# Turning a router product round inside a software-pipelined sweep: weights stationary, both halves of a tile in one moving operand, the result one step later

## What is computed

```python
# channel mixing, then the second residual's norm
r2 = sigmoid(einsum('btc,dc->btd', xr2, cm_Wr))
k2 = square(relu(einsum('btc,dc->btd', xk2, cm_Wk)))
x  = x + r2 * einsum('btc,dc->btd', k2, cm_Wv)
x  = x0 + ga * x                                  # residual, gated
h  = layernorm(x) * (1 + cb) + sb                 # "h3" in the kernel
# router of the experts
logits = einsum('bsd,ed->bse', h, Wr)             # 8 experts
scores = softmax(logits); topk_scores, topk_idx = top_k(scores, 2)
out = gb * (shared(h) + routed(h, topk_scores, topk_idx)) + x
```

## Time and profile before

| | |
|---|---|
| Time, median of 3 runs | 1969.69 us (1968.26 to 1974.74) |
| Span of the profiled execution | 1967.3 us |
| PE busy | 1751.4 us, 89% of the span |
| DVE busy | 1323.2 us, 67% |
| ACT busy | 716.7 us, 36% |
| POOL busy | 575.9 us, 29% |
| Channel mixing, 543 to 845 us | PE 276.67 us busy of 302, DVE 268.78, mean granted clock 0.89 |

### The profile page before, as it was taken

The page is one execution under the profiler, slowest core; times in us unless marked ns, Lnnn a source line. Parts: engine busy times, 40 slices in busy tenths (PEclk is TensorE's granted clock), DMA queues, the critical chain, the costliest instruction groups (busy, mean ns, idle before and its releaser), DMA issues.

```text
span 1967.3 us, 29963 instructions
## 1 busy us (share of the span) xinstructions
PE 1751.4 (89%) x9188; PEld 1523.2 (77%) x9188; DVE 1323.2 (67%) x2361; ACT 716.7 (36%) x1146; POOL 575.9 (29%) x691
## 2 busy tenths in 40 slices
PE   4599999997899999997999999999999999999800
PEld 0488888885777777776899999998999999999800
DVE  4899999965898898877432333326666666666566
ACT  2344444443433343333111111115554554554322
POOL 0343333323776676643144410000000000000076
PEclk8799999998998888887999999999999999999955
DMA  8333333327544334322455521105667767667387
GB/s 322 115 122 116 116 116 116 116 84 255 199 145 149 133 134 144 128 89 83 148 181 186 185 92 43 43 22 187 240 231 248 241 230 248 238 232 248 108 260 252
DMA packets 140152, 321.82 MB, mean 164 GB/s; under 512 B 20184, under 2 KB 20184, under 8 KB 134864
## 3 DMA queue, kind: packets, MB, share of 16 engines
q1 hardware_dynamic: 116080, 258.94, 39.4%
q0 software_dynamic: 12800, 41.95, 6.5%
q10 hardware_dynamic: 11232, 20.45, 2.7%
HBM read 213.23 MB, written 108.05 MB: 163 GB/s over the span
## 4 chain that ended last, share of the span: by engine, by line
PE 74%; DVE 14%; POOL 4%; issue 4%; DMA 3%; ACT 1%; SPq 0%; DVEq 0%; POOLq 0%; ACTq 0%
PE bank L424 17%; PE bank L426 17%; PE bank L425 17%; DVE mix L1280 5%; PE bank L1730 5%; PE bank L1728 5%; PE bank L1729 5%; PE bank L435 4%; POOL cb_y L863 3%; PE bank L1722 2%; DVE xh L1265 2%; DVE h_lo L1335 1%; PE bank L1678 1%; DMA stage<-in_w_k 1%; PE bank L1679 1%
## 5 line engine op out<-in xcount | busy, mean ns | idle before, releaser
L424 PE MATMUL bank<-gu_hi,ex_x_hi 128*128 128x352 f32 x1136 | 382.0, 336 | 0.8 <-DVE gu_lo L1362 0.8
L426 PE MATMUL bank<-gu_hi,ex_x_lo 128*128 128x352 f32 x1136 | 369.5, 325 | 0.0
L425 PE MATMUL bank<-gu_lo,ex_x_hi 128*128 128x352 f32 x1136 | 369.2, 325 | 0.0
L863 POOL DMA_INDIRECT cb_y<-expert_out_rows,slots x64 | 69.2, 1081 | 738.9 <-DMA expert_out_rows<-y_rows 719.7
L1478 DVE TENSOR_TENSOR hid<-bank,sg_t 128x352 f32<-128x352 f32 x142 | 74.5, 525 | 307.6 <-ACT sg_t L1015 307.6
L424 PEld LDWEIGHTS bank<-gu_hi,ex_x_hi 128*128 128x128 f32 x1136 | 216.1, 190 | 1.2 <-issue 1.2
L425 PEld LDWEIGHTS bank<-gu_lo,ex_x_hi 128*128 128x128 f32 x1136 | 216.1, 190 | 0.0
L426 PEld LDWEIGHTS bank<-gu_hi,ex_x_lo 128*128 128x128 f32 x1136 | 215.2, 189 | 0.0
L1015 ACT ACTIVATE sg_t<-bank 128x352 f32<-128x352 f32 x142 | 65.8, 464 | 396.6 <-PE bank L426 396.6
L1728 PE MATMUL bank<-dn_hi,hid_hi 128*128 128x512 f32 x426 | 168.0, 394 | 3.1 <-DVE hid_lo L1482 3.1
L1730 PE MATMUL bank<-dn_hi,hid_lo 128*128 128x512 f32 x426 | 168.2, 395 | 0.0
(11 more groups left out here) (214 smaller groups left out, 3999.8 us busy)
## 6 DMA issues: line engine op xcount, KB each, us to landing
raw<-in_ex_gu SPq DMA_DIRECT2D x39, 1408.0 KB, 6.6
expert_in_rows<-zero_rows SPq DMA_DIRECT2D x32, 624.0 KB
raw<-in_ex_dn SPq DMA_DIRECT2D x39, 512.0 KB, 7.5
ex_x<-expert_in_rows SPq DMA_DIRECT2D x78, 256.0 KB, 2.7
expert_out_rows<-y_rows ACTq DMA_DIRECT2D x78, 256.0 KB, 2.0
h_rows<-h_t SPq DMA_DIRECT2D x64, 256.0 KB, 2.6
x_t<-in_x SPq DMA_DIRECT2D x32, 256.0 KB, 2.8
timemix_rows<-o_t SPq DMA_DIRECT2D x32, 256.0 KB, 2.0
```

The source lines that it names most:

```text
L424: pe.matmul(acc, act_hi[i], w_hi[i], start=(i == 0), stop=False)
L425: pe.matmul(acc, act_hi[i], w_lo[i], start=False, stop=False)
L426: last = pe.matmul(acc, act_lo[i], w_hi[i], start=False, stop=(i == chunks - 1))
L863: pool.indirect_dma_start(rows[:, pair % 2, a, :], None, ys_d, bass.IndirectOffsetOnAxis(ap=slots[:, k, n:n + 1], axis=0)).then_inc(arrive ...
```

## The change

The router's product is turned round. The weights become the stationary operand: `wrt_hl` is now 128 columns wide (8 high, 8 low, 112 columns of zeros), and the tile's high and low halves lie beside each other in `h3_hl`, so that one chunk is one moving operand of 256 columns: 4 matmuls instead of 8. The result has experts on the partitions and 2 x 128 rows on the columns. ACT copies it to memory (`logits_by_expert`, a new stage), and a new PE stage, `by_row`, turns and adds it with two plain fp32 matmuls whose moving operand is `halves`, a 128x8 selection matrix. DVE then copies 8 columns, one instruction in place of two. `router` goes from lag 4 to lag 5, `by_row` has lag 6, `logits_out` goes from lag 5 to lag 6. The split of the router's weights moves from the set-up to the first steps of channel mixing (`router_zeros`, `router_hi`, `router_lo`, once each). At the end of the sweep PE itself waits for the last logits.

```diff
@@ tiles
-        wrt_hl = sb("wrt_hl", [P, C, 16], F32R)
+            lg_t = sb("lg_t", [P, 2, P], at=a2)
+            wrt_hl = sb("wrt_hl", [P, C, P], F32R, a2)
+            h3_hl = sb("h3_hl", [P, C, 2, P], F32R, a2)
+            h3_hi, h3_lo = h3_hl[:, :, 0, :], h3_hl[:, :, 1, :]
@@ POOL
+            pool.tensor_tensor(halves[:], ident[:, 0:E], ident[:, E:2 * E], ALU.add).then_inc(const_ready, 1)
...
+            def router_zeros(t):
+                if t.pair is None and t.n == 0:
+                    wait_a1(pool)
+                    pool.memset(wrt_hl[:, :, 2 * E:P].bitcast(F32), 0.0).then_inc(wrt_zero, 1)
@@ ACT
+            def logits_by_expert(t):
+                if t.back(1).real():
+                    act.wait_ge(*lg_pe.done(t.back(1).n, "by_row"))
+                act.wait_ge(*t3_pe.done(t.n, "logits"))
+                act.activation(flat(lg_t[:]), PS_LG[:, 0:2 * P], ACT.Copy).then_inc(lg_act.sem, 1)
-            sweep(act, NT, *in_turn((sr2_of, 0), (k2hi, 1), (h3hi, 4), (mix2_hi, -1), (k2_of, 0), (h2T_of, -2),
+            sweep(act, NT, *in_turn((sr2_of, 0), (logits_by_expert, 5), (router_hi, 2), (k2hi, 1), (h3hi, 4), (mix2_hi, -1), (k2_of, 0), (h2T_of, -2),
@@ DVE
             def logits_out(t):
-                dve.wait_ge(*t3_pe.done(t.n, "logits"))
-                dve.tensor_scalar(lg_part[:, t.p, :], PS_LG[:, 0:8], 1.0, None, ALU.mult).then_inc(lg_vec.sem, 1)
-                dve.wait_ge(*lg_vec.done(t.n, "part"))
-
-                dve.tensor_tensor(logits[:, bass.ds(t.n, 1), :].rearrange("p a e -> p (a e)"), lg_part[:, t.p, :],
-                                  PS_LG[:, 8:16], ALU.add).then_inc(lg_vec.sem, 1)
+                dve.wait_ge(*lg_pe.done(t.n, "by_row"))
+                dve.tensor_copy(logits[:, bass.ds(t.n, 1), :].rearrange("p a e -> p (a e)"),
+                                PS_LR[:, 0:E]).then_inc(lg_vec.sem, 1)
-            sweep(dve, NT, *in_turn((pads, 1), (y_of, 2), (logits_out, 5), (first_col_2, -1), (stats_3, 3), (stats_2, -3), (moments_3, 3), (xhat_2, -2),
+            sweep(dve, NT, *in_turn((pads, 1), (y_of, 2), (logits_out, 6), (router_lo, 3), (first_col_2, -1), (stats_3, 3), (stats_2, -3), (moments_3, 3), (xhat_2, -2),
@@ PE
             def router(t):
...
                 for c in range(C):
-                    pe.matmul(PS_LG[:, 0:16], h3_hi[:, c, :], wrt_hl[:, c, :], start=c == 0, stop=False)
-                    last = pe.matmul(PS_LG[:, 0:16], h3_lo[:, c, :], wrt_hl[:, c, :], start=False, stop=c == C - 1)
+                    last = pe.matmul(PS_LG[:, 0:2 * P], wrt_hl[:, c, :], h3_hl[:, c].rearrange("p h t -> p (h t)"),
+                                     start=c == 0, stop=c == C - 1)
                 last.then_inc(t3_pe.sem, 1)
+
+            def by_row(t):
+                if t.back(1).real():
+                    pe.wait_ge(*lg_vec.done(t.back(1).n, "copied"))
+                pe.wait_ge(*lg_act.done(t.n, "by_expert"))
+                pe.matmul(PS_LR[:, 0:E], lg_t[:, 0, :], halves[:], start=True, stop=False)
+                pe.matmul(PS_LR[:, 0:E], lg_t[:, 1, :], halves[:], start=False, stop=True).then_inc(lg_pe.sem, 1)
...
-            sweep(pe, NT, *in_turn((r2, 0), (tk, 1), (t3, 4), (k2, 0), (t2, -2), (router, 4), (cv, 1), (first_shared, 3)))
+            sweep(pe, NT, *in_turn((r2, 0), (by_row, 6), (router, 5), (tk, 1), (t3, 4), (k2, 0), (t2, -2), (cv, 1), (first_shared, 3)))
+            pe.wait_ge(*lg_vec.done(NT - 1, "copied"))
```

More of the change, by code:

```diff
@@ L162, in build @@
         wrt = sb("wrt", [P, C, 8])
-        wrt_hl = sb("wrt_hl", [P, C, 16], F32R)
-        wrt_hi, wrt_lo = wrt_hl[:, :, 0:8], wrt_hl[:, :, 8:16]
+        halves = sb("halves", [P, E])
         bridge_col = sb("bridge_col", [P, 4])
@@ L192, in build @@
         sr2 = sb("sr2", [P, 2, D], at=mixing)
-        h3_hi = sb("h3_hi", [P, C, P], F32R, mixing)
+        spare = sb("spare", [P, D], at=mixing)
         with ExitStack() as first:
@@ L247, in build @@
             rstd3 = sb("rstd3", [P, 2, 1], at=a2)
-            lg_part = sb("lg_part", [P, 2, 8], at=a2)
+            lg_t = sb("lg_t", [P, 2, P], at=a2)
+            wrt_hl = sb("wrt_hl", [P, C, P], F32R, a2)
+            wrt_hi, wrt_lo = wrt_hl[:, :, 0:E], wrt_hl[:, :, E:2 * E]
+            h3_hl = sb("h3_hl", [P, C, 2, P], F32R, a2)
+            h3_hi, h3_lo = h3_hl[:, :, 0, :], h3_hl[:, :, 1, :]
             pool_col = sb("pool_col", [P, 1], at=a2)
             h2T = sb("h2T", [P, 2, C, P + 1], at=a2)
-            h3_lo = sb("h3_lo", [P, C, P], F32R, a2)
         mixing.close()
@@ L284, in build @@
         gated_t = sb("gated_t", [P, D])
+        after_mixing = sb("after_mixing", [P, 2, D])
         hid_hi = sb("hid_hi", [P, FK, P], F32R)
@@ L380, in build @@
         t3_vec = steps("t3_vec", "h3_lo")
-        lg_vec = steps("lg_vec", "part", "copied")
+        wrt_zero = sem("wrt_zero")
+        wrt_hi_act = sem("wrt_hi_act")
+        wrt_lo_vec = sem("wrt_lo_vec")
+        lg_pe = steps("lg_pe", "by_row")
+        lg_act = steps("lg_act", "by_expert")
+        lg_vec = steps("lg_vec", "copied")
         zeroed = sem("zeroed")
@@ L442, in build @@
         PS_V = psum[5:7]
-        PS_R2, PS_K2, PS_CV, PS_T2, PS_TK, PS_T3, PS_LG = psum[0:7]
+        PS_R2, PS_K2, PS_CV, PS_T2, PS_TK, PS_T3, PS_LG, PS_LR = psum[0:8]
         def wait_h_rows(eng):
@@ L458, in build @@
         MOD_DONE = MOD_AT[-1]
-        CONSTS = 5
+        CONSTS = 6
         ROUTE_BOTH = 17
@@ L751, in _ @@
             pool.tensor_scalar(keep[:], keep_i[:], 0.0, None, ALU.is_gt).then_inc(const_ready, 1)
+            pool.wait_ge(const_ready, CONSTS - 1)
+            pool.tensor_tensor(halves[:], ident[:, 0:E], ident[:, E:2 * E], ALU.add).then_inc(const_ready, 1)
             pool.wait_ge(const_ready, CONSTS)
@@ L828, in rstd_3 @@
                 pool.tensor_tensor(rstd3[:, t.p, :], var2[:, 1:2], minus_half[:], ALU.pow).then_inc(ln3_pool.sem, 1)
-            sweep(pool, NT, *in_turn((diff_2, -1), (x3, 2), (rstd_3, 3), (rstd_2, -3), (gated, 2), (xres, 2), (x2, -4)))
+            sweep(pool, NT, *in_turn((diff_2, -1), (router_zeros, 1), (x3, 2), (rstd_3, 3), (rstd_2, -3), (gated, 2), (xres, 2), (x2, -4)))
             wait_a2(pool)
@@ L877, in _ @@
             act.wait_ge(vec_in, 160)
-            act.activation(wrt_hi, wrt[:], ACT.Copy).then_inc(wsplit_hi, 1)
             def h1T_of(t):
@@ L920, in _, with router_hi @@
             wait_h_rows(act)
+            def router_hi(t):
+                if t.pair is None and t.n == 0:
+                    wait_a1(act)
+                    act.activation(wrt_hi, wrt[:], ACT.Copy).then_inc(wrt_hi_act, 1)
             def h2T_of(t):
@@ L961, in h3hi @@
                 act.wait_ge(*t3_pe.done(t.n, "turned"))
-                act.activation(flat(h3_hi[:]), PS_T3[:], ACT.Copy).then_inc(t3_act.sem, 1)
+                act.activation(h3_hi, bank_chunks(PS_T3), ACT.Copy).then_inc(t3_act.sem, 1)
+            def logits_by_expert(t):
[3 more added lines that the diff above has]
+                act.activation(flat(lg_t[:]), PS_LG[:, 0:2 * P], ACT.Copy).then_inc(lg_act.sem, 1)
             def shared_x_hi(t):
@@ L1153, in split_last @@
                     split_lo(NW - 1)
-                    dve.wait_ge(wsplit_hi, NW + 1)
-                    dve.tensor_tensor(wrt_lo, wrt[:], wrt_hi.bitcast(F32), ALU.subtract).then_inc(wsplit_lo, 1)
+                    dve.wait_ge(vec_in, 160)
                     dve.wait_ge(u_in, 16)
-                    dve.wait_ge(wsplit_lo, NW + 1)
                     dve.tensor_scalar(u_bc[:], u_bc[:], LN_1E8, None, ALU.add).then_inc(u_ready, 1)
@@ L1334, in h3lo, with router_lo @@
                 dve.wait_ge(*t3_act.done(t.n, "h3_hi"))
-                dve.tensor_tensor(flat(h3_lo[:]), PS_T3[:], flat(h3_hi[:]).bitcast(F32),
+                dve.tensor_tensor(h3_lo, bank_chunks(PS_T3), h3_hi.bitcast(F32),
                                   ALU.subtract).then_inc(t3_vec.sem, 1)
-            def logits_out(t):
-                dve.wait_ge(*t3_pe.done(t.n, "logits"))
-                dve.tensor_scalar(lg_part[:, t.p, :], PS_LG[:, 0:8], 1.0, None, ALU.mult).then_inc(lg_vec.sem, 1)
-                dve.wait_ge(*lg_vec.done(t.n, "part"))
-                dve.tensor_tensor(logits[:, bass.ds(t.n, 1), :].rearrange("p a e -> p (a e)"), lg_part[:, t.p, :],
-                                  PS_LG[:, 8:16], ALU.add).then_inc(lg_vec.sem, 1)
+            def router_lo(t):
+                if t.pair is None and t.n == 0:
+                    wait_a1(dve)
+                    dve.wait_ge(wrt_hi_act, 1)
+                    dve.tensor_tensor(wrt_lo, wrt[:], wrt_hi.bitcast(F32), ALU.subtract).then_inc(wrt_lo_vec, 1)
+            def logits_out(t):
+                dve.wait_ge(*lg_pe.done(t.n, "by_row"))
+                dve.tensor_copy(logits[:, bass.ds(t.n, 1), :].rearrange("p a e -> p (a e)"),
+                                PS_LR[:, 0:E]).then_inc(lg_vec.sem, 1)
             def pads(t):
@@ L1605, in r @@
```

(13 more changed lines are left out.)

## The result

| | before | after |
|---|---|---|
| Median of the runs | 1968.97 us (4 runs, 1967.5 to 1974.74) | 2020.2 us (4 runs, 2016.02 to 2024.65) |
| Ratio | | 1.0251, 95% interval 1.0226 to 1.0276 |
| Span of the profiled execution | 1967.3 us | 2017.0 us |
| y of tile 4 to y of tile 27, 23 steps | 13.15 us a step | 15.09 us a step |

What follows compares the result with a forecast made beforehand. The prediction took a DVE-PE ring in channel mixing as the bound: 13.8 + 0.9 x 1.57 = 15.2 us a step against 13.15, over 26 steps +53 us, ends nothing, so 2023 us; range 1990 to 2056.

Steps and rivals of the forecast that it cites:

- The bound: Channel mixing: each step is a ring through DVE and PE, 13.15 us, though both engines look nearly full.
- The new wait: Channel mixing: DVE's logits copy waits for `by_row`, behind all of `r2`, 2 us or more in some 26 steps.
- The ring at full clock: Copy to `k_lo` 7.40, then 0.1, `cv` 2.86, `r2` 2.73, `by_row` 0.45, way to DVE 0.2: about 13.8 us.
- a dearer sum: `by_row` on PE counted as 8 passes at 0.11 us each, 0.4 us a step above the 0.45 taken.
- The clock: PE idles 2.8 to 3.2 us before `cv`; low clock in nine steps of ten, at least 1.57 us each.
- A sign that failed: Channel mixing's sweep: the mean granted clock was to fall below 0.89.
- The other signs: Copy waits 2+ us; y hardly; PE idles 3 us; steps 15.2 us; `r2` in chain; other stages within 2 us.
- The steps: Channel mixing, steps 6 to 31: 26 steps, each 2.05 us longer (15.2 for 13.15), +53 us.
- The sum: Whole program: 53 us added to the 1967.3 us span, 2020, and 2.4 us for the median: 2023 us.
- The rival on the other side: `by_row` costs no wait if `r2` is over when y begins: 11.7 us a step, 1937 us; 5 in 100.
- The first rival: Ring grows but clock holds in most steps: 13.8 to 14.2 us a step, 1987 to 1997 us; 17 in 100.

Runs made afterwards that it cites:

- e10: The kernel before with 4 idle products of 384 columns on PE between `t2` and the router, in the loop's steps: 1944.5 us, ratio 0.9886.
- e1: The changed kernel with `by_row` ahead of `r2` on PE instead of behind it: 1934.83 us, ratio 0.9828.
- e2: The changed kernel with DVE's copy of the logits one step later (lag 7 for 6), PE's order unchanged: 1937.07 us, ratio 0.9846.
- e3: The kernel before with its old router product moved from ahead of `cv` (lag 4) to behind `r2` (lag 5): 2071.35 us, ratio 1.0537.
- e5: The changed kernel with 12 idle products of 384 columns on PE between `t2` and `cv`, in the loop's steps: 1989.79 us, ratio 1.0107.
- e6: The changed kernel with the router's 4 matmuls ahead of `by_row`, both behind `r2`: 2066.27 us, ratio 1.0479.
- e7: The changed kernel with the turned router back ahead of `cv` (lag 4) and `by_row` at lag 5 behind `k2`: 1929.58 us, ratio 0.9785.
- e8: e6 with 12 idle products on PE between `t2` and `cv`, in the loop's steps: 2005.89 us, ratio 1.0191.
- e9: e3 with 12 idle products on PE between `t2` and `cv`, in the loop's steps: 2013.64 us, ratio 1.0237.
- e4: e3 with DVE's two logits instructions one step later (lag 6 for 5): 1948.88 us, ratio 0.9889.

## Why the prediction was right

*The bound.* Right. One step is a ring over DVE and PE, and a full PE says nothing: e10 puts more work on PE and is faster.

*The new wait.* Right, in place and kind: 27 waits for 26 counted, 2.4 us each. e1 and e2 take it away in two ways that share nothing, and e3 makes it out of the old kernel. This is shown.

*The ring at full clock.* Forecast 13.75 to 13.8, measured 13.83 in one step of the change and 13.78 over the whole of e5. Counted from start to start as the prediction did, the step of 13.83 us is 7.48 from the copy to the end of k_lo (696.08 to 703.56; 7.40 forecast), 0.13 to `cv`, 2.84 for `cv`, 2.73 for `r2`, and 0.65 for `by_row` with its way to DVE. Only inside the last were two terms off, and they cancelled: the four records of `by_row` stand 0.36 us end to end (709.26 to 709.62) where 0.45 was forecast, and the way to DVE takes 0.29 where 0.2 was. From the rule of the Trainium skill (FP8 and Floating Point Precision, "TensorE Precision Notes") that true fp32 takes four passes, the prediction had worked out a dearer sum, 0.4 us more a step. That sum does not hold; with 0.36 us for the whole of `by_row`, the number of passes itself can't be read from these records. Off the ring, the router's four wide matmuls take 0.56 us (709.62 to 710.18) for the 0.48 forecast.

*The clock.* Right in kind, near in size: 15.09 us a step for 15.2. Between y of tile 4 and y of tile 27 it fell in 20 of 23 steps, near the nine in ten forecast; the steps of 14.25, 14.15 and 13.61 us, which end with y at 707.22, 751.61 and 887.49, have a granted clock of 1.00. The 1.3 us a step that it costs are 1.5 for each step in which it fell, for 1.57 forecast. That this agrees is luck in part. The forecast price was that of `cv` alone at today's low stretch. In the change `cv` loses 1.1 to 1.5 us, and in every other such step `r2` loses 0.3 to 0.5 more (3.0 to 3.2 us for 2.73). e6, settled, pays 2.8 us a step for the same cause, and nothing in the prediction told which of the two prices it would be.

*A sign that failed.* The prediction expected the mean granted clock of the sweep to fall below 0.89. It is 0.90 over 543 to 845 us. Where the clock fell, the mean of a step is 0.87 before and 0.89 after: the step has become 1.9 us longer and its mean clock no lower. What the low clock costs is read from the products on the ring, not from the mean. The other signs came as named, except that the end of the program grew by more than 2 us (below).

*The steps.* 26 were counted, and the sum made with 2.05 us for each; 27 waits are there. Measured: y of tile 4 comes 2.4 us earlier than before (540.31 for 542.72), as forecast for the first steps; from there to tile 27 44.8 us are lost (23 times 1.95); from tile 27 to 31 2.5; to the first up-product of the shared experts, their first product, 1.3 more. Together the first up-product is 46 us later, 955.20 for 909.10, where the sum had 53.

*The sum.* 2023 forecast, 2020.2 measured, with two misses that partly cancel: up to the end of the sweep 46 us were lost for 53, and behind it 3.6 us (1061.8 for 1058.2) that no step had. The final gathers took 4.7 us longer (below). That these misses offset each other is luck.

*The rival on the other side.* Its reasoning was sound and its condition false in the change: e1 meets the condition and gives 11.60 us a step, where 11.7 was worked out, and 1935 us for 1937. *The first rival*, a clock that holds, is what e5 makes true with its idle products: 1990, inside its 1987 to 1997.

## What to carry to other kernels

In a software-pipelined sweep with a fixed order on each engine, ask of every moved stage not what it costs but which long stage now stands ahead of it in the same step, and who takes its result with what behind it. A consumer that reads the result one step later costs nothing but a lag; e2 is a change of one digit and turns a loss of 2.5% into a gain of 1.5%. Where PE waits a little in each step and its granted clock is under 1.00, look at what it does in the gap before looking at its work: idle matmuls there (e10) gave 24 us here, and wide ones in place of thin ones, with one DVE instruction less a step, 39 (e7; by e10 some 24 of these are the clock's, an estimate).

## What the runs showed of the hardware

Two rings that differ by 0.15 us at full clock (e8 14.3, e9 14.45) and lie 0.5 to 0.7 above that of the change fall to the same 17.1 us a step once their gap is left empty, where the change falls to 15.1. So a ring 0.5 us longer pays 2.7 us a step for the clock where the shorter one pays 1.3. The empty gap ahead of `cv` is 3.03 to 3.13 us in most steps of the change, 3.55 to 3.66 in e6 and 3.73 to 3.83 in e3. Why the price doubles just there was not tried.

The length of the gap alone does not decide. In the change 3.12 us stand empty ahead of `cv` at 703.69, as in its neighbours, and `cv` takes 2.84 us, all at full clock. The first gap of 2.84 us brings the clock down in the change (`cv` at 550.32 takes 4.14 us) and not in e5, which has no idle products yet there (`cv` at 552.39 takes 2.85). Before, 1.2 us of idle time with 0.9 us of 16-column matmuls behind it brought the clock down in 19 of these 23 steps, while 1.3 to 1.4 us without them did not in e4.

The final gathers by POOL are the same instructions in all kernels, and their stretch differs from one kernel's profiled execution to another's. The view of the tile `cb_y` (shortest, middle and longest in ns, then the first start and the last) in the kernel before, after, and in e6:

```profile
L863 POOL DMA_INDIRECT cb_y<-expert_out_rows,slots x64: 942/1062/1790, 1868.3 to 1954.9; - x64
```

```profile
L878 POOL DMA_INDIRECT cb_y<-expert_out_rows,slots x64: 942/1062/1794, 1913.5 to 2004.8; - x64
```

```profile
L878 POOL DMA_INDIRECT cb_y<-expert_out_rows,slots x64: 942/1066/1793, 1959.7 to 2056.4; - x64
```

86.6 us, 91.3 and 96.7; the first and the last are the ends of what all twelve profiles show. Each kernel has one profile, so it is not shown how much of this is chance. The 4.7 us between before and after are a tenth of the difference of their spans. A change to an early stage of this kernel is read more exactly at a mark behind that stage than in the span.
